# A conv/attention block with a dense mixture of experts: the experts' first layer in f32 on four 64x64 quadrants instead of two f16 halves on 128x64

## The chip, the cores and the metric

The kernel runs on one core of a Trainium2 chip. The metric is device time in microseconds of one execution; lower is better. Three runs of the kernel before took 228.62, 228.63 and 231.39 us, median 228.63 us.

## The reference

x is (4, 64, 64, 16) f32: four images, a column axis of 64 rows (h), and 64 x 16 positions. The first part (a cosine transform, windowed attention, convolutions, inverse transform) gives x1, which is added to x. The second part treats each of the 4 x 1024 positions as a token of 64 features. What the change touches is this second part:

```python
logits = xt @ Wr + br
probs = jax.nn.softmax(logits, axis=-1)
top_p, top_idx = jax.lax.top_k(probs, TOP_K)          # TOP_K = 2
weights = top_p / top_p.sum(axis=-1, keepdims=True)
...
xn = (xt - mu) * jax.lax.rsqrt(var + LN_EPS)
xe = xn[None, :, :] * ln_g[:, None, :] + ln_b[:, None, :]
h = jax.nn.gelu(jnp.einsum('end,edh->enh', xe, W1) + b1[:, None, :], approximate=False)
y = jnp.einsum('enh,ehd->end', h, W2) + b2[:, None, :]
```

There are 8 experts, each 64 -> 256 -> 64. The kernel computes all 8 for every token and weighs them by a gate that is zero for the unchosen ones.

## The kernel before, in words

**Layout.** The four images are two pairs. A pair lies with image and h on the 128 partitions (image 0 on rows 0 to 63, image 1 on rows 64 to 127) and 1024 positions on the free axis. Four "steps" of 512 positions (`CHUNK`) times 8 experts make 32 *units* `u`.

**Order.** `TURN` gives each stage of the first part a turn for pair 0 and for pair 1, and `in_turn` sorts them; every engine walks its own list in that order and waits on semaphores. The units come at turns 90, 100, 110 and so on: `experts(r)` on TensorE first does the second layer of units 2r and 2r+1 (`down`), then the first layer of units 2r+4 and 2r+5 (`up`), since `AHEAD` is 2. Rounds r = -2 and r = -1 have no `down`. Between them, at turns 91 to 94, stand pair 1's `router`, `features`, `keep_tokens` and `tanh_gap`; after r = -1 come `gates_to_rows` and `keep_gates` (101, 102), and SyncE then sends the gates through DRAM and back, copied over the partitions (`store_gates`, `load_gates`).

**First layer before.** A unit has four *tiles* `t`: two halves of the hidden axis (`k`) for each of two images (`b`), each a PSUM bank of 128 hidden rows by 512 tokens. The tokens are split into an f16 high part and an f16 low part, which lie above each other on the 128 partitions (`tok`), so one 128-row matmul multiplies both with the same f16 weights; the weights too are split in two f16 parts (`w1s`), which are accumulated. `up` (L675 to L697) thus issues per tile 2 parts x 2 column sides = 4 f16 matmuls of 128 rows by 64 columns by 512. The split costs `high_part` on ScalarE (L818), `low_part` on GpSimdE (L922), f16 transposes in `features` (L638), copies of 128x1024 f16 in `keep_tokens` (L830), and two more operations in `weights_of_first` (L935, L936).

**Banks.** The first layer has two PSUM banks in the first four units (`h_early`, rounds r = -2 and r = -1, 16 tiles) and six afterwards (`h_late`). Before each tile, `up` waits for the Gelu of the last tile that used this bank. `gelu_hidden` on ScalarE (L852) reads a tile, adds the bias and writes `hid_of[u % 4]`. ScalarE is the only reader.

**Second layer.** `down` (L699) is four f32 matmuls of 128 rows by 64 columns by 512 per unit; VectorE multiplies the result by the gate and adds it (`add_expert`, L1160 and L1165).

An f32 matmul is one row in the order of instructions and two in the trace (two passes); an f32 transpose is one.

Of the kernel before, what the change touches and what calls it, by code (L numbers as in the profile page):

```python
# [15 lines left out]
P = 128  # L16
PAIRS, B2, H, W, C = 2, 2, 64, 64, 16
K = 8
# [4 lines left out]
E, HID = 8, 256  # L23
# [29 lines left out]
    "inverse_over_kh": (35, 40), "keep_back": (24, 27), "keep_half": (25, 28), "square_tokens": (26, 31),  # L53
    "mix_branches": (16, 18), "inverse_over_kw": (36, 41), "high_part": (29, 92), "tokens": (37, 43),
    "residual": (19, 22), "norm_tokens": (21, 24), "keep_tokens": (30, 93), "features": (42, 92), "low_part": (6, 7),
    "router": (39, 91), "route": (23, 25), "gates_to_rows": (101, 102), "shares": (26, 27), "biases": (20, 20),
# [32 lines left out]
def constants():  # L89

    def twice(a):
        return np.kron(np.eye(2), a)
    n = np.arange(H)
    angle = np.cos(np.pi * (2 * n[None, :] + 1) * n[:, None] / (2 * H))
    dct = 2.0 * angle
    weight = np.ones(H)
    weight[0] = 0.5
    idct = (weight[:, None] * angle / H).T
    centred = dct - dct.mean(axis=1, keepdims=True)
    centred[1:] = dct[1:]  # L100
# [19 lines left out]
    return out, np.eye(P, dtype=np.float16)  # L120

# [36 lines left out]

def metaformer(nc, x, small, W1, W1T, ln_b, W2, const32, const16, out):
    ctx = ExitStack()  # L160
    with ctx:
# [36 lines left out]
        c32 = sb("c32", [P, CONST_N])  # L198
        c16 = sb("c16", [P, P], F16)

# [4 lines left out]
        mask = c32[:, CONST["shifted"].start + C:CONST["shifted"].start + C + P]  # L205
        ident16 = c16[:, 0:P]
        sm = sb("sm", [P, SMALL_N])
# [16 lines left out]
        w1g = sb("w1g", [P, E, HID])  # L224
        w1s = sb("w1s", [P, 2, E, HID], F16)
        w2 = sb("w2", [P, NT, H])
# [6 lines left out]
        x1 = sb("x1", [P, PAIRS, N])  # L233
        tok = sb("tok", [P, PAIRS, 2, B2, TT // 2 * P], F16)
        still = sb("still", [P, CHUNK], F16)
# [19 lines left out]
        back = x_conv  # L255
        parts = [x_conv[p].bitcast(F16) for p in range(PAIRS)]
        h2 = [place[4][:, p, :] for p in range(PAIRS)]
# [31 lines left out]

        hid = sb("hid", [P, 2, TILES, CHUNK])  # L290
        hid_of = [hid[:, 0], hid[:, 1]] + [w[:, :, :].rearrange("p (t a) n -> p t (a n)", t=TILES) for w in (w1f, w1g)]
        gate_b = [wide[n][:, 0, :].rearrange("p (e n) -> p e n", n=CHUNK) for n in range(2)]
# [4 lines left out]
        gate_store = nc.dram_tensor("gate_store", (PAIRS, 2, B2, E * CHUNK), F32)  # L297

        def part_of(p, part, j):

            return parts[p].rearrange("p (t a h) -> p t a h", a=2, h=H)[:, j * K:(j + 1) * K, part, :]

        def shifted(p, b, tap):
# [5 lines left out]
        dct_in = sem("dct_in")  # L309
        const_in, const16_in, weights_in = sem("const_in"), sem("const16_in"), sem("weights_in")  # L310
        ffn_in, out_done = sem("ffn_in"), sem("out_done")
# [18 lines left out]
         attn_ready, y_ready, yt_ready, mix_ready, xout_ready, back_ready, half_ready, x1_ready, csq_ready, xn_ready,  # L330
         high_ready, parts_ready, wr_centred_ready, logits_read, tok_ready, gap_ready, tanh_ready, gparts_ready, gates_ready, coef_ready) = (sem(n) for n in (
             "sq_ready dh_ready dw_ready xd_ready h1_ready halo_ready xt_ready gram_ready prod_ready tk_ready "
             "dconv_ready xconv_ready spread_ready scaled_ready h2_ready rest_ready logit_ready exp_ready "
             "attn_ready y_ready yt_ready mix_ready xout_ready back_ready half_ready x1_ready csq_ready xn_ready "
             "high_ready parts_ready wr_centred_ready logits_read tok_ready gap_ready tanh_ready gparts_ready gates_ready coef_ready").split())

# [9 lines left out]
        def _(sp):  # L346
# [5 lines left out]
            sp.dma_start(xs[:, 1, :], xv[1]).then_inc(x_in[1], 16)  # L352
            sp.dma_start(c16[:, :], const16).then_inc(const16_in, 16)
            w1v = W1.rearrange("e d n -> d e n")
# [53 lines left out]
        def _(pe):  # L408
# [229 lines left out]
            def features(p):  # L638

                pe.wait_ge(const16_in, 16)  # L640
                pe.wait_ge(logits_read, p + 1)
                to = slot(p, 1).bitcast(F16)
                for j in range(TT):
                    if j % 4 == 0:
                        pe.wait_ge(parts_ready, 2 * p + j // 4 + 1)
                    for b in range(B2):
                        a = (j // 4 * 2 + b) * CHUNK + j % 4 * P
                        mm = pe.transpose(to[:, a:a + P], parts[p][:, (j * 2 + b) * P:(j * 2 + b + 1) * P], ident16)
                    if j % 4 == 3:
                        mm.then_inc(tok_done, 1)  # L650
# [24 lines left out]
            def up(u):  # L675
# [8 lines left out]
                if u == EARLY:  # L684
                    pe.wait_ge(gates_ready, PAIRS)
                for t in range(TILES):
                    k, b = divmod(t, B2)
                    n = TILES * u + t
                    before = last_in(h_bank, n)
                    if before >= 0:  # L690
                        pe.wait_ge(gelu_ready, before + 1)
                    for part in range(2):
                        for side in range(2):
                            mm = pe.matmul(h_bank(n)[side * H:(side + 1) * H, :],  # L694
                                           w1s[:, part, e, k * P + side * H:k * P + (side + 1) * H], tok[:, pair, half, b, :],
                                           start=part == 0, stop=part == 1)
                    mm.then_inc(w1_done, 1)  # L697

# [32 lines left out]
        def _(act):  # L731
# [85 lines left out]

            def high_part(p):  # L818
                for j in range(2):
                    act.wait_ge(xn_ready, 2 * p + j + 1)  # L820
                    act.copy(part_of(p, 0, j), split(bank(xc[p], j), H)).then_inc(high_ready, 1)  # L821

            def keep_router_weights(p):
# [28 lines left out]
            def gelu_hidden(u):  # L852
# [4 lines left out]
                for t in range(TILES):  # L857
# [6 lines left out]
            stages = (square_columns, keep_router_weights, keep_dw, keep_xd, gelu_in, keep_xt, keep_tk, gelu_depthwise, gelu_out, exponent,  # L864
                      keep_y, keep_yt, keep_back, keep_half, square_tokens, high_part, keep_tokens, tanh_gap, keep_gates)
            for stage, args in in_turn(stages, experts):
# [4 lines left out]
        def _(pool):  # L871
# [49 lines left out]

            def low_part(p):  # L922

                for j in range(2):
                    pool.wait_ge(high_ready, 2 * p + j + 1)
                    pool.tensor_tensor(part_of(p, 1, j), split(bank(xc[p], j), H), part_of(p, 0, j), ALU.subtract).then_inc(parts_ready, 1)  # L926

            def weights_of_first(p):
# [9 lines left out]
            for stage, (p,) in in_turn((weights_of_first, join, high, low_part)):  # L938
                stage(p)
# [252 lines left out]
```

## Time and profile before

| | us |
|---|---|
| median of three runs | 228.63 |
| profiled execution, span from first to last instruction | 227.4 |
| run median less this span | 1.2 |
| TensorE busy | 206.7 (91%) |
| ScalarE busy | 128.1 (56%) |
| VectorE busy | 123.8 (54%) |
| GpSimdE busy | 47.0 (21%) |
| TensorE's share of the chain that ended last | 68% |
| mean granted TensorE clock | 0.981 |

The profile's own record of the execution has no other time than its span, so the 1.2 us between it and the median of the runs is taken as what lies around the span. "PE" is TensorE's matmuls, "PEld" its weight loads, DVE is VectorE, ACT is ScalarE, POOL is GpSimdE. A matmul record (start, duration) lasts longer than the distance to the next one, since matmuls are pipelined: distances between starts give the rate. The chain of waits is followed back from the last instruction and shows what set the end.

### The profile page before, as it was taken

The numbers are of one execution on the slowest core, as the hardware profiler recorded it, in microseconds if no ns is written. First come the engines' busy times: TensorE is split into PE (matmuls) and PEld (weight loads), VectorE is DVE, ScalarE is ACT, GpSimd is POOL, SyncE is SP. The second block draws the span as 40 slices with busy tenths as digits, with TensorE's granted clock in tenths as the row PEclk, the third lists the DMA queues.
The fourth block names the chain that finished last, engine by engine and source line by source line (L and its number), as shares of the span: only waits on it lengthen the run. The fifth ranks groups of instructions, "written<-read, shape, count | busy, mean of one in ns | idle before, by whom it ended". The sixth has DMA issues, their size and how long they took to land.

```text
span 227.4 us, 4913 instructions
## 1 busy us (share of the span) xinstructions
PE 206.7 (91%) x2096; PEld 113.6 (50%) x2096; DVE 123.8 (54%) x232; ACT 128.1 (56%) x207; POOL 47.0 (21%) x50
## 2 busy tenths in 40 slices
PE   7699788999976898988899799999999999999993
PEld 3395667566334577963524244444444444444430
DVE  0582055659949977999731633554334553334555
ACT  2256942035338553669685387666786666786640
POOL 5560393040069992030400000000000000000000
PEclk9979999999999999999699999999999999999998
DMA  6990000000000000000005953260804508063001
GB/s 219 294 265 14 0 3 6 3 0 7 0 0 4 0 3 0 3 0 0 3 0 164 220 128 69 82 151 0 184 3 108 122 4 184 0 150 84 0 0 46
DMA packets 6596, 14.35 MB, mean 63 GB/s; under 512 B 2736, under 2 KB 4144, under 8 KB 5680
## 3 DMA queue, kind: packets, MB, share of 16 engines
q1 hardware_dynamic: 6576, 14.06, 24.7%
q8 instruction: 16, 0.26, 0.5%
q14 instruction: 4, 0.03, 0.0%
HBM read 12.87 MB, written 1.18 MB: 62 GB/s over the span
## 4 chain that ended last, share of the span: by engine, by line
PE 68%; ACT 9%; DMA 7%; POOL 6%; DVE 6%; SPq 1%; issue 1%; POOLq 1%; DVEq 0%
PE psum L710 22%; PE psum L694 21%; PE psum L538 7%; DMA xs<-in_x 3%; DMA wide<-gate_store 2%; PE psum L512 2%; POOL place L920 2%; ACT place L747 2%; PE psum L634 2%; PE psum L548 2%; PE psum L424 2%; POOL place L926 2%; ACT hid L861 1%; POOL place L919 1%; PE psum L557 1%
## 5 line engine op out<-in xcount | busy, mean ns | idle before, releaser
L694 PE MATMUL psum<-tok,w1s 128*64 128x512 f16 x512 | 60.8, 383 | 1.3 <-ACT hid L861 0.8
L1160 DVE SCALAR_TENSOR_TENSOR term<-psum,sm,wide 128x512 f32<-128x512 f32 x32 | 24.0, 750 | 62.1 <-PE psum L710 51.6
L861 ACT ACTIVATE hid<-psum,b1p 128x512 f32<-128x512 f32 x64 | 38.2, 701 | 16.7 <-PE psum L694 16.3
L694 PEld LDWEIGHTS psum<-tok,w1s 128*64 128x64 f16 x512 | 28.7, 110 | 35.9 <-issue 9.1
L861 ACT ACTIVATE w1f<-psum,b1p 128x512 f32<-128x512 f32 x32 | 19.6, 688 | 17.1 <-PE psum L694 17.0
L710 PE MATMUL psum<-hid,w 128*64 128x512 f32 x128 | 28.9, 593 | 0.0
L1165 DVE TENSOR_TENSOR x<-x,term 128x512 f32<-128x512 f32 x32 | 22.1, 692 | 1.1
L861 ACT ACTIVATE w1g<-psum,b1p 128x512 f32<-128x512 f32 x32 | 19.7, 714 | 0.2
L710 PEld LDWEIGHTS psum<-hid,w 128*64 128x64 f32 x128 | 9.1, 137 | 15.1 <-issue 9.4
L710 PE MATMUL psum<-w1g,w 128*64 128x512 f32 x64 | 15.1, 594 | 1.4 <-DVE term L1160 1.4
L538 PE MATMUL psum<-h_pad,tap_bd 64*64 64x512 f32 x144 | 15.9, 589 | 0.0
L710 PE MATMUL psum<-w1f,w 128*64 128x512 f32 x64 | 15.1, 594 | 0.1
L777 ACT ACTIVATE place<-psum 128x512 f32<-128x512 f32 x4 | 2.2, 594 | 15.4 <-PE psum L538 15.4
L538 PEld LDWEIGHTS psum<-h_pad,tap_bd 64*64 64x64 f32 x144 | 6.8, 133 | 7.5 <-issue 7.5
L911 POOL TENSOR_TENSOR place<-place 128x1024 f32<-128x1024 f32 x2 | 4.7, 2353 | 26.0 <-ACT place L777 26.0
L710 PEld LDWEIGHTS psum<-w1g,w 128*64 128x64 f32 x64 | 4.5, 137 | 10.9 <-issue 6.6
L414 PE MATMUL psum<-still 128*128 128x512 f16 x28 | 8.0, 435 | 1.3 <-POOL still L872 1.3
L926 POOL TENSOR_TENSOR place<-place 128x512 f16<-128x512 f32 x4 | 4.6, 1166 | 19.7 <-ACT place L821 19.7
L998 DVE TENSOR_TENSOR wide<-psum,sm 128x1024 f32<-128x1024 f32 x4 | 4.7, 1220 | 7.0 <-PE psum L498 7.0
L735 ACT ACTIVATE place<-psum 128x512 f32<-128x512 f32 x4 | 2.4, 597 | 10.3 <-PE psum L424 10.3
L710 PEld LDWEIGHTS psum<-w1f,w 128*64 128x64 f32 x64 | 4.5, 137 | 6.7 <-issue 3.1
L992 DVE TENSOR_TENSOR wide<-psum,c 128x512 f32<-128x512 f32 x4 | 2.6, 682 | 9.6 <-PE psum L486 9.6
(147 smaller groups left out, 295.4 us busy)
## 6 DMA issues: line engine op xcount, KB each, us to landing
wide<-gate_store SPq DMA_DIRECT2D x14, 512.0 KB, 6.4
xs<-in_x SPq DMA_DIRECT2D x2, 512.0 KB, 5.6
w1f<-in_W SPq DMA_DIRECT2D x2, 512.0 KB, 10.0
block_out<-x SPq DMA_DIRECT2D x4, 256.0 KB, 6.4
wide<-gate_store SPq DMA_DIRECT2D x2, 384.0 KB, 5.1
c<-const SPq DMA_DIRECT2D x1, 548.5 KB, 4.4
hid<-in_W1T SPq DMA_DIRECT2D x1, 512.0 KB, 10.3
w<-in_W SPq DMA_DIRECT2D x1, 512.0 KB, 11.8
```

The lines of the kernel that those rows point to most:

```text
L414: pe.matmul(where, still[:, 0:P], still[:, 0:where.shape[1]], start=True, stop=True)
L424: mm = pe.matmul(slot(p, 0)[:, cp * P:(cp + 1) * P], xs[:, p, cp * P:(cp + 1) * P], dct_h, start=True, stop=True)
L512: mm = pe.matmul(bank(slot(p, 0), swapped)[rows_of(crossed(half, swapped)), 0:side], const("pick")[rows_of(half), first:first + H], column ...
L538: mm = pe.matmul(bank(slot(p, 0), b)[rows_of(crossed(half, b)), :], tap_bd[rows_of(half), tap, :], shifted(p, b, tap)[rows_of(half)], star ...
L694: mm = pe.matmul(h_bank(n)[side * H:(side + 1) * H, :], w1s[:, part, e, k * P + side * H:k * P + (side + 1) * H], tok[:, pair, half, b, :] ...
L710: mm = pe.matmul(y_bank(u)[b * H:(b + 1) * H, :], w2[:, e * KT + k, :], hid_of[u % 4][:, B2 * k + b, :], start=k == 0, stop=k == KT - 1)
L861: act.activation(hid_of[u % 4][:, t, :], h_bank(n), ACT.Gelu, bias=b1p[:, e * KT + k:e * KT + k + 1]).then_inc(gelu_ready, 1)
L911: pool.tensor_tensor(x_conv[p], x_conv[p], xd[p], ALU.add).then_inc(xconv_ready, 1)
L926: pool.tensor_tensor(part_of(p, 1, j), split(bank(xc[p], j), H), part_of(p, 0, j), ALU.subtract).then_inc(parts_ready, 1)
L998: dve.tensor_tensor(prod[p].rearrange("p (s o q) n -> p o s q n", s=2, o=2)[:, j], slot(p, j).rearrange("p (s q n) -> p s q n", s=2, n=P), ...
L1160: dve.scalar_tensor_tensor(term[:, u % 2, :], y_bank(u), b2t[:, e:e + 1], gate_b[part][:, e % (E // 2), :], ALU.add, ALU.mult).then_inc(te ...
L1165: dve.tensor_tensor(x1p, x1p, term[:, u % 2, :], ALU.add).then_inc(add_done, 1)
```

## The change

The tokens stay f32 in the pair's layout: image 0's 64 features on rows 0 to 63, image 1's on rows 64 to 127. The first layer is then, for each k, four f32 matmuls of 64 rows by 64 columns by 512: image by row half, side of the hidden half by column half, with the order (image 0, side 0), (image 1, side 1), (image 0, side 1), (image 1, side 0). `high_part`, `low_part`, `w1s` and the constant `c16` go; `tok` is f32; `features` is 8 f32 transposes for a pair instead of 16 f16 ones; `keep_tokens` copies 128x512 f32. Since `w1g` now stays as the weights, the fourth hidden buffer is a third part of `hid`. `up` waits for both banks of a k before its first matmul.

```diff
-                for t in range(TILES):
-                    k, b = divmod(t, B2)
-                    n = TILES * u + t
-                    before = last_in(h_bank, n)
-                    if before >= 0:
-                        pe.wait_ge(gelu_ready, before + 1)
-                    for part in range(2):
-                        for side in range(2):
-                            mm = pe.matmul(h_bank(n)[side * H:(side + 1) * H, :],
-                                           w1s[:, part, e, k * P + side * H:k * P + (side + 1) * H], tok[:, pair, half, b, :],
-                                           start=part == 0, stop=part == 1)
-                    mm.then_inc(w1_done, 1)
+                moving = bank(tok[:, pair, :], half)
+                for k in range(KT):
+                    first = TILES * u + B2 * k
+                    for b in range(B2):
+                        before = last_in(h_bank, first + b)
+                        if before >= 0:
+                            pe.wait_ge(gelu_ready, before + 1)
+                    for swapped in range(2):
+                        for b in range(B2):
+                            side = crossed(b, swapped)
+                            mm = pe.matmul(h_bank(first + b)[rows_of(side), :],
+                                           w1g[rows_of(b), e, k * P + side * H:k * P + (side + 1) * H], moving[rows_of(b), :],
+                                           start=True, stop=True)
+                            if swapped:
+                                mm.then_inc(w1_done, 1)
...
-                pe.wait_ge(const16_in, 16)
                 pe.wait_ge(logits_read, p + 1)
-                to = slot(p, 1).bitcast(F16)
                 for j in range(TT):
                     if j % 4 == 0:
-                        pe.wait_ge(parts_ready, 2 * p + j // 4 + 1)
-                    for b in range(B2):
-                        a = (j // 4 * 2 + b) * CHUNK + j % 4 * P
-                        mm = pe.transpose(to[:, a:a + P], parts[p][:, (j * 2 + b) * P:(j * 2 + b + 1) * P], ident16)
+                        pe.wait_ge(xn_ready, 2 * p + j // 4 + 1)
+                    mm = pe.transpose(slot(p, 1)[:, j * P:(j + 1) * P], xc[p][:, j * P:(j + 1) * P], ident)
...
-                act.copy(tok[:, p, j, :, :].rearrange("p b n -> p (b n)"),
-                         slot(p, 1).bitcast(F16)[:, j * N:(j + 1) * N]).then_inc(tok_ready, 1)
+                act.copy(bank(tok[:, p, :], j), bank(slot(p, 1), j)).then_inc(tok_ready, 1)
...
-                link(pool.tensor_tensor(w1g[:, :, :], w1f[:, :, :], lng.unsqueeze(2).broadcast_to([P, E, HID]), ALU.mult))
-                link(pool.tensor_copy(w1s[:, 0, :, :], w1g[:, :, :]))
-                pool.tensor_tensor(w1s[:, 1, :, :], w1g[:, :, :], w1s[:, 0, :, :], ALU.subtract).then_inc(w1_ready, 1)
+                pool.tensor_tensor(w1g[:, :, :], w1f[:, :, :], lng.unsqueeze(2).broadcast_to([P, E, HID]), ALU.mult).then_inc(w1_ready, 1)
```

**TensorE from pair 1's `tokens` through round r = -2 to pair 1's `features`, before** (`psum<-c,x` is `tokens`, `psum<-tok,w1s` the first layer, L666 the router, L648 `features`):

```order
L634 MATMUL psum<-c,x 128x128 [waits x1_ready]
L634 MATMUL psum<-c,x 128x128 x3
L694 MATMUL psum<-tok,w1s 64x512 [waits tok_ready,w1_ready,bias_ready]
L694 MATMUL psum<-tok,w1s 64x512 x7
L694 MATMUL psum<-tok,w1s 64x512 [waits gelu_ready]
L694 MATMUL psum<-tok,w1s 64x512 x3
L666 MATMUL psum<-wr_centred,x 128x16 [waits wr_centred_ready,x1_ready]
L666 MATMUL psum<-wr_centred,x 128x16 x7
L648 MATMUL psum<-c,place 128x128 [waits parts_ready,logits_read,const16_in]
L648 MATMUL psum<-c,place 128x128 x7
```

The pair of rows with the wait for `gelu_ready` stands six times there, once for each tile from the third on. With the change:

```order
L625 MATMUL psum<-c,x 128x128 [waits x1_ready]
L625 MATMUL psum<-c,x 128x128 x3
L683 MATMUL psum<-tok,w1g 64x512 [waits tok_ready,w1_ready,bias_ready]
L683 MATMUL psum<-tok,w1g 64x512 x3
L683 MATMUL psum<-tok,w1g 64x512 [waits gelu_ready]
L683 MATMUL psum<-tok,w1g 64x512 x3
L653 MATMUL psum<-wr_centred,x 128x16 [waits wr_centred_ready,x1_ready]
L653 MATMUL psum<-wr_centred,x 128x16 x7
L635 MATMUL psum<-c,place 128x128 [waits xn_ready,logits_read]
L635 MATMUL psum<-c,place 128x128 x3
```

The pair with `gelu_ready` now stands three times, and each stands for two tiles.

**ScalarE over the same stretch, before** (L821 is `high_part`, L833 `keep_tokens`, L816 `square_tokens`, L861 the Gelu, L838 `tanh_gap`):

```order
L821 CAST place<-place 128x8x64 [waits xn_ready] x2
L833 COPY tok<-psum 128x1024 [waits tok_done] x2
L816 ACTIVATE place<-psum 128x512 [waits tokens_done] x2
L861 ACTIVATE hid<-psum,b1p 128x512 [waits w1_done] x8
L838 ACTIVATE st<-st 128x16 [waits gap_ready]
L821 CAST place<-place 128x8x64 [waits xn_ready] x2
L833 COPY tok<-psum 128x1024 [waits tok_done] x2
L838 ACTIVATE st<-st 128x16 [waits gap_ready]
L861 ACTIVATE w1f<-psum,b1p 128x512 [waits w1_done] x4
```

And with the change:

```order
L818 COPY tok<-psum 128x512 [waits tok_done] x2
L806 ACTIVATE place<-psum 128x512 [waits tokens_done] x2
L845 ACTIVATE hid<-psum,b1p 128x512 [waits w1_done] x8
L822 ACTIVATE st<-st 128x16 [waits gap_ready]
L818 COPY tok<-psum 128x512 [waits tok_done] x2
L822 ACTIVATE st<-st 128x16 [waits gap_ready]
L845 ACTIVATE hid<-psum,b1p 128x512 [waits w1_done] x4
```

The casts are gone; pair 1's tanh still stands ahead of the Gelus of round r = -1, and eight Gelus still stand ahead of pair 0's tanh.

## Rows read from the trace of the kernel before

**Rows 1.** Chain of waits, in order of time: start us, us, what.

```profile
130.54 3.45 PE psum L694 x32
133.99 3.43 PE psum L710 x16
...
216.63 6.89 PE psum L710 x32
```

**Rows 2.** Timeline, TensorE, pair 1's taps: start us, us, engine line, operation.

```profile
55.36 7.92 PE L538 MATMUL psum<-h_pad,tap_bd 64*64 64x512 f32 x72
```

**Rows 3.** Groups by line: busy us, mean ns, idle before and its releaser.

```profile
L538 PE MATMUL psum<-h_pad,tap_bd 64*64 64x512 f32 x144 | 15.9, 589 | 0.0
```

**Rows 4.** Timeline, ScalarE, the eight Gelus of one steady round.

```profile
151.73 4.74 ACT L861 ACTIVATE hid<-psum,b1p 128x512 f32<-128x512 f32 x8 [2.15 <-PE psum L694]
```

**Rows 5.** Timeline, TensorE, changes between 64x64, 128x64 and 128x128 tiles.

```profile
28.76 1.09 PE L458 MATMUL psum<-place,enter_bd 64*64 64x512 f32 x8 [0.66 <-ACT place L747]
29.77 1.14 PE L465 MATMUL psum<-place,conv_bd 128*64 128x64 f32 x16
48.58 1.98 PE L548 MATMUL psum<-wide,c 128*128 128x512 f32 x4
50.49 2.10 PE L512 MATMUL psum<-wide,c 64*64 64x64 f32 x128
```

**Rows 6.** Timeline, TensorE, pair 1's inverse transform to pair 1's router.

```profile
95.56 2.00 PE L625 MATMUL psum<-c,place 128*128 128x128 f32 x16
...
99.73 2.00 PE L634 MATMUL psum<-c,x 128*128 128x128 f32 x16
101.66 1.05 PE L694 MATMUL psum<-tok,w1s 128*64 128x512 f16 x8
...
107.01 1.96 PE L666 MATMUL psum<-wr_centred,x 128*128 128x16 f32 x16
```

**Rows 7.** Chain of waits, from pair 0's features to the gates' arrival.

```profile
91.13 0.87 PE psum L608 x8
...
96.95 2.28 POOL place L926 x2
...
103.73 0.70 ACT hid L861
104.43 0.04 issue
104.47 0.64 PE psum L694 x4
105.12 0.02 issue
...
117.18 1.30 ACT w1g L861 x2
118.48 0.18 ACT gate_rows L843 x2
...
127.80 0.76 DVE term L1160
128.60 1.94 PE psum L710 x8
```

**Rows 8.** Timeline, ScalarE, pair 1's tanh and round r = -1.

```profile
112.85 0.22 ACT L838 ACTIVATE st<-st 128x16 f32<-128x16 f32 x1
112.97 2.70 ACT L861 ACTIVATE w1f<-psum,b1p 128x512 f32<-128x512 f32 x4
```

**Rows 9.** Busy us by stretch: PE, PEld, DVE, ACT, POOL, granted clock, DMA share, GB/s.

```profile
7.40:10.80 3.40, 1.20 (x7) 0.51 (x5) 2.35 (x6) 0.00 (x0) 2.34 (x8) 1.00 1.08 259
62.00:65.40 3.40, 2.13 (x14) 0.64 (x7) 1.72 (x2) 1.08 (x2) 0.92 (x1) 1.00 0.00 0
106.40:109.80 3.40, 2.57 (x23) 2.04 (x22) 2.43 (x6) 2.40 (x6) 1.30 (x2) 0.99 0.00 0
109.80:113.20 3.40, 3.34 (x24) 2.04 (x24) 3.09 (x10) 2.27 (x4) 1.01 (x1) 0.50 0.02 5
```

More of the change, by code:

```diff
@@ L53 @@
     "inverse_over_kh": (35, 40), "keep_back": (24, 27), "keep_half": (25, 28), "square_tokens": (26, 31),
-    "mix_branches": (16, 18), "inverse_over_kw": (36, 41), "high_part": (29, 92), "tokens": (37, 43),
-    "residual": (19, 22), "norm_tokens": (21, 24), "keep_tokens": (30, 93), "features": (42, 92), "low_part": (6, 7),
+    "mix_branches": (16, 18), "inverse_over_kw": (36, 41), "tokens": (37, 43),
+    "residual": (19, 22), "norm_tokens": (21, 24), "keep_tokens": (30, 93), "features": (42, 92),
     "router": (39, 91), "route": (23, 25), "gates_to_rows": (101, 102), "shares": (26, 27), "biases": (20, 20),
@@ L119, in constants @@
     out[:, CONST["small_index"]] = np.arange(E, 0, -1)[None, :]
-    return out, np.eye(P, dtype=np.float16)
+    return out
 SMALL = {}
@@ L156, in small_weights, with metaformer @@
     return out
-def metaformer(nc, x, small, W1, W1T, ln_b, W2, const32, const16, out):
+def metaformer(nc, x, small, W1, W1T, ln_b, W2, const32, out):
     ctx = ExitStack()
@@ L233, in metaformer @@
         x1 = sb("x1", [P, PAIRS, N])
-        tok = sb("tok", [P, PAIRS, 2, B2, TT // 2 * P], F16)
+        tok = sb("tok", [P, PAIRS, N])
         still = sb("still", [P, CHUNK], F16)
@@ L255, in metaformer @@
         back = x_conv
-        parts = [x_conv[p].bitcast(F16) for p in range(PAIRS)]
         h2 = [place[4][:, p, :] for p in range(PAIRS)]
@@ L288, in last_in @@
             return max((k for k in range(n) if which(k) is which(n)), default=-1)
-        hid = sb("hid", [P, 2, TILES, CHUNK])
-        hid_of = [hid[:, 0], hid[:, 1]] + [w[:, :, :].rearrange("p (t a) n -> p t (a n)", t=TILES) for w in (w1f, w1g)]
+        hid = sb("hid", [P, 3, TILES, CHUNK])
+        hid_of = [hid[:, 0], hid[:, 1], hid[:, 2], w1f[:, :, :].rearrange("p (t a) n -> p t (a n)", t=TILES)]
         gate_b = [wide[n][:, 0, :].rearrange("p (e n) -> p e n", n=CHUNK) for n in range(2)]
@@ L297, in metaformer @@
         gate_store = nc.dram_tensor("gate_store", (PAIRS, 2, B2, E * CHUNK), F32)
-        def part_of(p, part, j):
-            return parts[p].rearrange("p (t a h) -> p t a h", a=2, h=H)[:, j * K:(j + 1) * K, part, :]
         def shifted(p, b, tap):
@@ L309, in metaformer @@
         dct_in = sem("dct_in")
-        const_in, const16_in, weights_in = sem("const_in"), sem("const16_in"), sem("weights_in")
+        const_in, weights_in = sem("const_in"), sem("weights_in")
         ffn_in, out_done = sem("ffn_in"), sem("out_done")
@@ L330, in metaformer @@
          attn_ready, y_ready, yt_ready, mix_ready, xout_ready, back_ready, half_ready, x1_ready, csq_ready, xn_ready,
-         high_ready, parts_ready, wr_centred_ready, logits_read, tok_ready, gap_ready, tanh_ready, gparts_ready, gates_ready, coef_ready) = (sem(n) for n in (
+         wr_centred_ready, logits_read, tok_ready, gap_ready, tanh_ready, gparts_ready, gates_ready, coef_ready) = (sem(n) for n in (
              "sq_ready dh_ready dw_ready xd_ready h1_ready halo_ready xt_ready gram_ready prod_ready tk_ready "
@@ L816, in square_tokens @@
                     act.activation(bank(squares[p], j), bank(slot(p, 0), j), ACT.Square).then_inc(csq_ready, 1)
[L818 to L821, printed above, removed]
             def keep_router_weights(p):
@@ L864, in _ @@
             stages = (square_columns, keep_router_weights, keep_dw, keep_xd, gelu_in, keep_xt, keep_tk, gelu_depthwise, gelu_out, exponent,
-                      keep_y, keep_yt, keep_back, keep_half, square_tokens, high_part, keep_tokens, tanh_gap, keep_gates)
+                      keep_y, keep_yt, keep_back, keep_half, square_tokens, keep_tokens, tanh_gap, keep_gates)
             for stage, args in in_turn(stages, experts):
@@ L920, in high @@
                     pool.tensor_tensor(bank(rest[p], b), bank(h2[p], b), bank(xd[p], b), ALU.add).then_inc(rest_ready, 1)
[L922 to L926, printed above, removed]
             def weights_of_first(p):
@@ L933, in weights_of_first @@
                 pool.wait_ge(xt_ready, 1)
-                link(pool.tensor_tensor(w1g[:, :, :], w1f[:, :, :], lng.unsqueeze(2).broadcast_to([P, E, HID]), ALU.mult))
-                link(pool.tensor_copy(w1s[:, 0, :, :], w1g[:, :, :]))
-                pool.tensor_tensor(w1s[:, 1, :, :], w1g[:, :, :], w1s[:, 0, :, :], ALU.subtract).then_inc(w1_ready, 1)
-            for stage, (p,) in in_turn((weights_of_first, join, high, low_part)):
+                pool.tensor_tensor(w1g[:, :, :], w1f[:, :, :], lng.unsqueeze(2).broadcast_to([P, E, HID]), ALU.mult).then_inc(w1_ready, 1)
+            for stage, (p,) in in_turn((weights_of_first, join, high)):
                 stage(p)
@@ L1178 @@
     a = {n: np.asarray(v) for n, v in inputs.items()}
-    const32, const16 = constants()
+    const32 = constants()
     arrays = {
@@ L1184 @@
         "in_ln_b": a["L0_ffn_ln_b"].reshape(1, E * H), "in_W2": a["L0_ffn_W2"],
-        "const32": const32, "const16": const16,
+        "const32": const32,
     }
```

6 lines of the change are left out of this document (1 added, 5 removed).

## The prediction

> **What bounds the kernel now.** I read the chain of waits first, then the timelines of TensorE and ScalarE along it, then the busy table by stretch for the clock. From 130.54 us on it is TensorE alone: first layer of two units, 3.45 us, second layer of two units, 3.43 us, by turns, up to two second-layer blocks at the end [rows 1]. ScalarE does the eight Gelus of such a round in 4.74 us and then idles 2.15 us until TensorE delivers again [rows 4]. So late in the kernel only TensorE's rate counts. Before that the chain is another one: between 103 and 118.5 us it alternates between a Gelu on ScalarE (0.70 us) and a tile on TensorE (0.64 us) with 0.06 us of issue, 1.40 us for each turn [rows 7]. There the first layer has two PSUM banks, and each bank's turn is "matmul, then Gelu"; two banks in turn give a tile every 0.70 us. That chain leads to the copies of the gates at 118.48 us, their way through DRAM, and the first gated sum at 127.80 us, which frees TensorE at 128.60 us [rows 7]. Whatever delays the gates moves all that follows.
>
> **Steady rounds: the rate of the matmuls.** What is an f32 matmul on one quadrant worth? The taps are just that: 72 passes of 64x64 by 512 in 7.92 us [rows 2]. With four quadrants at work that is 18 slots; 7.92 less the 0.16 us by which one record (0.589) outlasts a slot gives 0.43 us a slot [rows 2, 3]. The second layer's 16 passes, two column halves at a time, are 8 slots in 3.43 us, 0.43 us as well [rows 1]. The first layer now needs, for two units, 16 f32 matmuls = 32 passes = 8 slots = 3.44 us. Before, 32 f16 passes, two at a time, took 3.45 us [rows 1]. The number of passes is the same; an f32 pass takes twice an f16 one, and four instead of two run side by side. **0.0 us** for each first-layer block after the early rounds.
>
> **Changes of tile shape.** All expert matmuls were 128x64. Now the first layer is 64x64 and the second stays 128x64, so the shape changes twice a round. Where this happens before: L458 starts at 28.76 and the next shape at 29.77, 1.01 us for two slots that should be 0.86, so 0.15 over; L548 takes 1.91 us to the next shape's start for four slots, 1.72, so 0.19 over [rows 5]. From the second layer at 128.60 us to the end there are 13 first-layer blocks, each with a change on both sides: 26. I take 0.15, from the row with 64-column weights, which is nearest: **+3.9 us**, with 0 and 26 x 0.19 = 4.9 as ends. The Trainium skill, "TensorEngine Tiling (Array Packing)", section Key Properties, says that a change of tiling mode, not of tile, drains TensorE. The rows agree in that a change is not free; if the 0.16 us tail of a record came on top of the 0.15 us, the sum would be 4.2 us higher, which is a rival below.
>
> **Steady bank waits.** `up` now waits for both banks of a pair. The fourth pair of a block needs the block's first two Gelus. They are ready 1.09 us (the pair's matmuls, [rows 5]) plus some 0.1 plus 1.30 us (two Gelus, [rows 7]) after the block's start, 2.5 us; the fourth pair is due at 3 x 0.86 + 0.15 = 2.73. Slack 0.2 us, so 0 us; if it fails, 13 x 0.2 is the price. Eight Gelus of 4.74 us still fit into a round of 7.2 us.
>
> **Pair 0's tokens.** ScalarE's casts and GpSimdE's two subtractions (2.28 us, in the chain [rows 7]) go. Eight f32 transposes, by L608 0.87 us [rows 7], can follow L625, which ends at 97.56 [rows 6]; then `tokens` of pair 1 takes 101.66 - 99.73 = 1.93 us as before. Round r = -2 starts at 100.36 instead of 101.66: **-1.3 us**. `keep_tokens` copies shorter rows beside it and is covered by these 1.93 us. GpSimdE's two missing weight operations end by some 45 us before and nobody waits: 0. One small DMA less at the start: 0.
>
> **Early rounds: both banks at once.** Here is the loss. With two banks and a pair of tiles per step, the overlap between TensorE and ScalarE is gone: a step is two Gelus 1.30 (from 117.18, [rows 7]), issue 0.04, a pair of tiles on four quadrants alone 1.09 (L458, two slots and the tail, [rows 5]), issue 0.02: **2.45 us for two tiles** instead of 1.40.
> - Round r = -2: the fourth pair starts at 100.36 + 3 x 2.45 = 107.71, pair 1's router 1.01 us later [rows 5], 108.72 instead of 107.01 [rows 6]: +1.7.
> - VectorE's routing of pair 1 is released by the router, and the tanh by that; ScalarE stands at this tanh, so the tanh moves from 112.85 to 114.55 and the first Gelu of round r = -1 from 112.97 to 114.7 [rows 8]. Pair 1's features, without the subtractions, lie in that time (1.0 us of transposes, two copies) and cost nothing.
> - Round r = -1: 114.7 + 1.30 + 3 x 2.45 = 123.35, and there the gates are copied, 118.48 before [rows 7]: **+4.9 us** against before, the -1.3 included. The DMAs, the first gated sum and the start at 128.60 shift with it. TensorE meanwhile does r = 0's second layer and the next first layer and waits again, as before.
>
> **Clock.** The granted clock was 1.00 in all but two places: it was 0.50 after 7.4 to 10.8 us, where PE was busy 1.20 of 3.40 us, and again at 109.8 to 113.2 us, after a stretch with the router's 16-column matmuls. It held 1.00 through 62.0 to 65.4 us with PE busy 2.13 of 3.40 [rows 9]. In the early steps PE will be busy 1.09 of every 2.45 us, more than before the first fall and less than where it held, and PE waits over 2 us on ScalarE, which stands at the tanh, within r = -1. I expect the lower level (1.2 GHz) once or twice more. At it two slots take up to 0.86 us longer; one low stretch like that of 109.8 to 113.2 holds one or two steps, so 0.9 to 1.7: **+1.3 us**, ends 0 and 5.2 (six steps).
>
> **Sum.** 227.4 + 4.9 + 3.9 + 1.3 = 237.5 us of span. The median of the runs lies 1.2 us over the profiled span of 227.4, so **238.7 us**, 4.4% over 228.63.
>
> **Rivals.**
> 1. *The clock stays at 2.4 GHz in the early rounds.* For it speaks that TensorE works every 2.45 us. 237.4 us, chance 0.28.
> 2. *It is low through both early rounds.* The rows allow it, since the new step lies between the one that fell and the one that held. 227.4 + 4.9 + 3.9 + 5.2 + 1.2 = 242.6 us, 0.12.
> 3. *Not slower: the early pair costs no overlap.* Place: the wait for `gelu_ready` ahead of each pair in rounds r = -2 and -1. The gates' delay is 6 x step - 9.8 us; if TensorE could fill one bank of a pair while the other is read, the step stayed 1.40 and the delay would be -1.4: 227.4 - 1.4 + 3.9 + 1.2 = 231.1 us, +1.1%. It decides below a step of 1.75 us. Against it: both waits stand ahead of the pair's first matmul, in the order of instructions too, and both banks get their last matmul in the same slot. 0.07. With free changes of shape besides, 227.2 us.
> 4. *A change of shape costs a whole drain on top.* 26 x (0.15 + 0.16) = 8.1 us in place of 3.9: 242.9 us. Against it: the over-long intervals above already contain the change. 0.05.
> 5. *The quadrants don't run four at a time.* Two at a time would add 14 x 3.44 = 48 us: 287 us. The taps run in the same four-quadrant order with the same passes, so 0.01.
> 6. *Faster by over 2%*, from something I don't see in ScalarE or the DMA of the gates: 0.02.
>
> My forecast's own case has the remaining 0.45. The **range** is 235.0 to 243.0 us: below it lies rival 3, above it 5 and little of 2 and 4; the lower end allows changes of 0.10 us (-1.3) and some 1 us of the early delay hidden. A measurement of this kernel can tell some 2% from no change, 4.6 us. Faster 0.02, within 2% 0.08, slower 0.90.
>
> **What would show it.** The chain after: first-layer blocks of about 3.6 us and second-layer ones of about 3.6 us, with no ScalarE in the steady part. Early rounds: TensorE groups 2.45 us apart, ScalarE Gelus in twos, and idle ScalarE of about 1.1 us between. Gates copied near 123 us. Granted clock 0.50 somewhere in 103 to 122 us. I am wrong if the steady first-layer block is not 3.4 to 3.7 us, if steps are under 2 us, or if ScalarE stands in the chain in the steady rounds (then the 0.2 us slack failed).

## The result and the profile after

| | kernel before | changed kernel |
|---|---|---|
| median of the runs, us | 228.62 (228.38 to 231.39, 4 runs) | 242.17 (241.60 to 243.27, 4 runs) |
| ratio, 95% interval | | 1.057 (1.051 to 1.063) |
| profiled execution, span, us | 227.4 | 239.8 |
| mean granted clock | 0.981 | 0.962 |

The changed kernel is 5.7% slower. The forecast was 238.7 us with a range of 235.0 to 243.0. Here and below a ratio leaves out runs that lie more than 1.5% above the kernel's fastest, so for own bank and for the common wait on the kernel before, it is not the quotient of the medians.

The chain of waits of the changed kernel over the early rounds and into the steady ones (start us, us, what; L683 is the first layer, L653 the router, L1067 VectorE's reading of the router's result, L635 the features, L845 the Gelu, L700 the second layer):

```profile
99.04 1.09 PE psum L683 x8
100.13 1.26 ACT hid L845 x2
101.39 0.14 issue
101.53 1.15 PE psum L683 x8
...
106.61 1.09 PE psum L683 x8
107.69 2.49 PE psum L653 x16
...
110.21 0.30 DVE place L1067
...
110.55 1.97 PE psum L635 x8
112.52 1.99 PE psum L683 x8
114.51 1.26 ACT hid L845 x2
...
115.90 2.05 PE psum L683 x8
...
124.81 1.25 ACT w1f L845 x2
126.06 0.18 ACT gate_rows L827 x2
...
135.86 0.76 DVE term L1136
...
136.66 1.94 PE psum L700 x8
138.60 3.63 PE psum L683 x32
142.23 3.58 PE psum L700 x16
...
228.81 7.04 PE psum L700 x32
```

Against [rows 7] the single Gelus have become twos, each with a whole pair of tiles behind it, and a step of two tiles takes 2.54 us in round r = -2 (101.53 to 104.06 in the timeline below) and 3.43 us in round r = -1 (115.90 to 119.34), where the pair's matmuls take 2.05 instead of 1.15 us. Between the two rounds the chain goes from the router through pair 1's features (L635) and the first pair of tiles to the first Gelu, all on TensorE but for 0.30 us on VectorE. Against [rows 1] a steady round has grown from 3.45 + 3.43 = 6.88 us to 3.63 + 3.58 = 7.21. ScalarE stands nowhere in the steady chain; its timeline there answers to [rows 4], the same 4.74 us and a longer idle time:

```profile
175.80 4.74 ACT L845 ACTIVATE hid<-psum,b1p 128x512 f32<-128x512 f32 x8 [2.48 <-PE psum L683]
```

The timeline of TensorE of the changed kernel over the same stretch (start us, us, engine, line, operation, idle before) answers to [rows 6]:

```profile
101.53 1.09 PE L683 MATMUL psum<-tok,w1g 64*64 64x512 f32 x8 [1.46 <-ACT hid L845]
104.06 1.09 PE L683 MATMUL psum<-tok,w1g 64*64 64x512 f32 x8 [1.45 <-ACT hid L845]
...
107.62 2.54 PE L653 MATMUL psum<-wr_centred,x 128*128 128x16 f32 x16
...
119.34 1.98 PE L683 MATMUL psum<-tok,w1g 64*64 64x512 f32 x8 [1.45 <-ACT hid L845]
```

Its busy table (busy us of PE, PEld, DVE, ACT, POOL, then the granted clock, DMA share, GB/s) shows where the longer pairs come from:

```profile
103.70:107.10 3.40, 1.58 (x15) 0.47 (x16) 2.21 (x7) 1.49 (x3) 0.00 (x0) 1.00 0.00 0
108.50:109.00 0.50, 0.50 (x6) 0.50 (x5) 0.00 (x0) 0.50 (x2) 0.00 (x0) 0.81 0.00 0
111.10:124.70 13.60, 9.24 (x40) 2.35 (x38) 4.82 (x20) 5.19 (x9) 0.00 (x0) 0.50 0.00 1
136.66:235.80 99.14, 99.14 (x648) 29.13 (x648) 42.36 (x59) 61.59 (x104) 0.00 (x0) 1.00 0.33 77
```

The granted clock falls between 108.5 and 109.0 us, within the router's matmuls and after a round in which TensorE idled 1.45 us in every step, and stays at 0.50 (1.2 GHz) until 125.5 us. Before, it was at 0.50 there from 109.8 to 113.2 us only [rows 9], and the first Gelu of round r = -1 started at 112.97 us [rows 8] instead of 114.51.

The two profiled executions differ by 12.4 us. Place by place, from the starts in the chains and timelines:

| stretch | before | after | difference, us |
|---|---|---|---|
| start to pair 1's inverse transform | 95.56 | 94.39 | -1.2 |
| from there to round r = -2 | 6.10 | 4.58 | -1.5 |
| round r = -2 to the router | 5.35 | 8.65 | +3.3 |
| router to the first Gelu of r = -1 | 5.96 | 6.87 | +0.9 |
| that Gelu to the gates' copy | 5.51 | 11.57 | +6.1 |
| gates' copy to the second layer of unit 3 | 10.12 | 10.60 | +0.5 |
| from there to the last gated sum | 94.95 | 99.21 | +4.3 |

The first row is not put down to the change: in the execution of before the clock was low during the first transform (16 matmuls there took 3.55 us), in that of after it was not (2.05 us), and spans of before measured later lie between 225.6 and 229.3 us.

### The profile page after: what moved, and what is told of

It is laid out like the page before. It is cut to its first block, busy times and chain, and to the rows that moved or that the text cites. A ratio compares the mean times of both kernels' runs of the same rounds, so it can differ in the third digit from the quotient of the medians.

```text
span 239.8 us, 4928 instructions
## 1 busy us (share of the span) xinstructions
PE 213.4 (89%) x2080; PEld 100.8 (42%) x2080; DVE 122.2 (51%) x232; ACT 124.4 (52%) x203; POOL 36.4 (15%) x44
## 4 chain that ended last, share of the span: by engine, by line
PE 70%; ACT 8%; DVE 7%; DMA 6%; POOL 3%; issue 2%; SPq 1%; POOLq 1%; DVEq 0%
PE psum L683 25%; PE psum L700 22%; PE psum L529 6%; ACT hid L845 3%; DMA wide<-gate_store 3%; DMA sm<-in_small 2%; PE psum L653 2%; PE psum L503 2%; ACT place L737 2%; PE psum L539 2%; PE psum L625 2%; POOL place L903 1%; PE psum L548 1%; PE psum L635 1%; PE psum L489 1%
## 5 line engine op out<-in xcount | busy, mean ns | idle before, releaser
L845 ACT ACTIVATE hid<-psum,b1p 128x512 f32<-128x512 f32 x96 | 57.7, 696 | 45.7 <-PE psum L683 45.7
L683 PE MATMUL psum<-tok,w1g 64*64 64x512 f32 x512 | 64.1, 630 | 8.7 <-ACT hid L845 7.3
L700 PE MATMUL psum<-hid,w 128*64 128x512 f32 x192 | 44.8, 603 | 0.4 <-DVE term L1136 0.4
L683 PEld LDWEIGHTS psum<-tok,w1g 64*64 64x64 f32 x512 | 17.0, 136 | 52.7 <-issue 27.2
L700 PEld LDWEIGHTS psum<-hid,w 128*64 128x64 f32 x192 | 12.5, 138 | 31.2 <-issue 29.2
L845 ACT ACTIVATE w1f<-psum,b1p 128x512 f32<-128x512 f32 x32 | 19.6, 714 | 4.3 <-PE psum L683 4.3
L700 PE MATMUL psum<-w1f,w 128*64 128x512 f32 x64 | 15.1, 594 | 1.5 <-DVE term L1136 1.5
L700 PEld LDWEIGHTS psum<-w1f,w 128*64 128x64 f32 x64 | 4.5, 137 | 10.9 <-issue 8.3
L904 POOL TENSOR_TENSOR place<-place 128x512 f32<-128x512 f32 x4 | 6.9, 1727 | 0.3
L903 POOL TENSOR_TENSOR place<-place,coef_rest 128x512 f32<-128x512 f32 x4 | 6.3, 1576 | 0.3
L902 POOL TENSOR_TENSOR place<-place 128x512 f32<-128x512 f32 x4 | 5.6, 1396 | 0.4 <-ACT place L772 0.4
L912 POOL TENSOR_TENSOR w1g<-w1f,sm 128x2048 f32<-128x2048 f32 x1 | 3.6, 3608 | 10.7 <-ACT place L755 10.7
```

The lines of the kernel that those rows point to most:

```text
L683: mm = pe.matmul(h_bank(first + b)[rows_of(side), :], w1g[rows_of(b), e, k * P + side * H:k * P + (side + 1) * H], moving[rows_of(b), :], ...
L700: mm = pe.matmul(y_bank(u)[b * H:(b + 1) * H, :], w2[:, e * KT + k, :], hid_of[u % 4][:, B2 * k + b, :], start=k == 0, stop=k == KT - 1)
L845: act.activation(hid_of[u % 4][:, t, :], h_bank(n), ACT.Gelu, bias=b1p[:, e * KT + k:e * KT + k + 1]).then_inc(gelu_ready, 1)
L902: link(pool.tensor_tensor(bank(h2[p], b), bank(h2[p], b), bank(x_conv[p], b), ALU.add))
L903: link(pool.tensor_tensor(bank(h2[p], b), bank(h2[p], b), coef_rest[:, :], ALU.mult))
L904: pool.tensor_tensor(bank(rest[p], b), bank(h2[p], b), bank(xd[p], b), ALU.add).then_inc(rest_ready, 1)
```

## The experiments

The theory was: the early rounds lose 10 us (3.3, 0.9 and 6.1 in the table) because both banks are waited for, filled and read together, part of it through the lower clock that TensorE's idling brings; and the steady rounds lose 4.3 us to changes of tile shape. The rivals: f32 quadrants are slow as such, or the order of waits costs in the steady rounds too. Each run was timed beside runs of the kernel before on the same chip; ratios are to that kernel.

### Fillers, for the clock

```diff
                     first = TILES * u + B2 * k
+                    if u < EARLY and (u % 2 or k):
+                        hold_clock(5, bank(slot(0, 0), 0))
```

> The changed kernel with five f16 matmuls of zeros (128x128 by 512) ahead of every wait for a pair of banks in the early rounds r = -2 and r = -1, on a PSUM bank that is free there; nothing else is changed. Theory (the clock follows TensorE's idle time): in the changed kernel the granted clock is 0.50 from pair 1's router to the gates' copies and a step of two tiles takes 3.43 us there instead of 2.54. With the fillers (some 1.1 us of the 1.45 us that TensorE idles in a step) the clock stays at 1.00, all steps take about 2.55, the router 1.9 and the gates are copied about 5 us sooner: about 237 us, 2% under the changed kernel. Rival (the low clock is an accident of this execution, or comes from f32 quadrants as such): the steps of round r = -1 stay at 3.4 us with the clock at 0.50, and the time stays at 241 to 243 us.

Measured: 238.92 us (237.67 to 241.06), ratio 1.044 (1.035 to 1.053); four executions with mean clocks of 0.982, 0.982, 0.993 and 1.000 and spans of 238.5, 237.5, 235.6 and 234.7. The timeline of its TensorE in round r = -1:

```profile
115.62 1.09 PE L685 MATMUL psum<-tok,w1g 64*64 64x512 f32 x8 [0.29 <-ACT hid L847]
116.64 1.25 PE L405 MATMUL psum<-still 128*128 128x512 f16 x5
118.16 1.09 PE L685 MATMUL psum<-tok,w1g 64*64 64x512 f32 x8 [0.27 <-ACT hid L847]
```

Steps are 2.54 us instead of 3.43, and the gates are copied at 123.10 us instead of 126.06. All four mean clocks lie above those of the changed kernel's four executions (0.948 to 0.968). So the low clock in the steps came from idling; f32 quadrants as such run at full clock, in the steady rounds too. The expectation was too good: the clock did not stay at 1.00 and the gates came 3.0 us sooner, not 5. The profiled execution still has a low stretch between the router and the first pair of round r = -1 (0.50 from 111 to 114 us) and one after the wait for the first gated sum, so the fillers mend a part, and what is left without any low clock (the execution at 1.000, span 234.7) is still far over the kernel before.

### Each image behind its own bank

```diff
                     for b in range(B2):
                         before = last_in(h_bank, first + b)
                         if before >= 0:
                             pe.wait_ge(gelu_ready, before + 1)
-                    for swapped in range(2):
-                        for b in range(B2):
-                            side = crossed(b, swapped)
+                        for side in range(2):
...
-                            if swapped:
-                                mm.then_inc(w1_done, 1)
+                        mm.then_inc(w1_done, 1)
```

> The changed kernel with another order inside a pair: wait for image 0's bank, its two column sides, then wait for image 1's bank, its two column sides. Only the order of matmuls and waits is changed. Theory (the pair's common wait is what costs in the early rounds): each bank goes round by itself, matmuls 1.09, Gelu 0.70, issue 0.16, about 1.95 us for two tiles instead of 2.54 to 3.43, the gates come 6 x 0.6 = 3.6 us sooner, and more if the clock stays up: 234 to 239 us. In the steady rounds the four quadrants still overlap, since passes on different quadrants overtake each other in the trace of the taps, so a block stays at 3.63 us. Rival 1 (TensorE starts passes strictly in program order): two passes of one quadrant block the next quadrant, only two quadrants overlap and steady blocks grow by up to 3.4 us each, up to 290 us. Rival 2 (the early delay comes from the f32 passes and not from the common wait): steps stay over 2.4 us and the time stays near 242.

Measured: 238.65 us over all four runs (235.97 to 240.35), ratio 1.033 (1.022 to 1.043). Its chain in round r = -2, then in the steady part:

```profile
99.92 0.70 ACT hid L842
100.62 0.04 issue
100.67 1.10 PE psum L681 x4
...
102.53 1.10 PE psum L681 x4
...
133.24 3.59 PE psum L681 x32
```

A step is 1.86 us (100.67 to 102.53) instead of 2.54, so waiting for, filling and ending both banks together costs 0.68 of the 1.14 us by which a step had grown over 1.40, and rival 2 falls. The gates are copied at 120.63 us. The profiled execution is the fastest of the four; their spans are 234.0, 235.0, 238.3 and 238.3 us at mean clocks of 0.978, 0.971, 0.950 and 0.947, and the ratio stands for the first two alone (over all four it is 1.043). The clock is low in this kernel too: the last two steps of the profiled execution took about 2.65 us each. The steady block stays at 3.59 us: rival 1 falls, four passes still run side by side.

### Four banks in the early rounds

```diff
-        h_early = [bank(slot(0, 1), 0), bank(slot(0, 1), 1)]
-        h_late = h_early + [bank(slot(1, 1), 0), bank(slot(1, 1), 1), bank(slot(1, 0), 1), bank(slot(0, 0), 0)]
+        h_early = [bank(slot(0, 1), 0), bank(slot(0, 1), 1), bank(slot(0, 0), 0), y_banks[0]]
+        h_late = h_early[:2] + [bank(slot(1, 1), 0), bank(slot(1, 1), 1), bank(slot(1, 0), 1), h_early[2]]
...
                 pe.wait_ge(gparts_ready, p + 1)
+                pe.wait_ge(gelu_ready, EARLY * TILES)
```

> The changed kernel with four PSUM banks for the first layer in the early rounds instead of two (the two more are pair 0's other slot, free there); the gates' transposes then wait for the sixteenth Gelu. Theory (bank turns bound the early rounds): TensorE fills one pair of banks while ScalarE reads the other, a step is two Gelus, 1.21 to 1.27 us, and round r = -2 and r = -1 are bound by ScalarE; the gates are copied some 8 to 11 us sooner, which includes the clock staying at 1.00 more of the time: 231 to 235 us. Rival (f32 passes or changes of tile shape bound the early rounds, not the banks): steps stay over 2 us and the gain is under 3 us, 239 to 242 us.

Measured: 231.04 us (229.58 to 232.11, 10 runs), ratio 1.008 (1.004 to 1.012). ScalarE's timeline of round r = -2, then the chain up to the gates and in the steady part:

```profile
100.03 4.96 ACT L846 ACTIVATE hid<-psum,b1p 128x512 f32<-128x512 f32 x8 [0.44 <-PE psum L684]
```

```profile
105.99 0.21 DVE place L1068
106.20 0.04 issue
106.25 1.97 PE psum L635 x8
108.22 1.66 PE psum L684 x8
...
114.83 0.14 issue
114.97 0.32 PE psum L661
115.31 0.29 ACT gate_rows L828 x2
...
127.30 3.63 PE psum L684 x32
```

Eight Gelus take 4.96 us, 1.24 us for two tiles: within a round ScalarE is now the bound. Round r = -2 is no longer in the chain at all: up to 106.20 us that runs over VectorE (normalising pair 1's tokens and, L1068, reading its router's result), which the expectation did not name. The gates are copied 10.75 us sooner than in the changed kernel, and 11 of its 13.5 us of loss are gone. This includes the clock: the ten executions have mean clocks of 0.992 to 1.000, and the changed kernel's low stretch had cost 3.6 us. From the start of round r = -2 to the gates' copy it now is 16.42 us, against 27.09 in the changed kernel and 16.82 in the kernel before. What remains, 1% (2.2 us), is about the steady rounds' 4.3 us less these 0.4 and the 1.5 us gained with pair 0's tokens.

### The common wait alone, put on the kernel before

```diff
-                    before = last_in(h_bank, n)
-                    if before >= 0:
+                    before = last_in(h_bank, n + 1 - b)
+                    if b == 0 and before >= 0:
```

> The kernel before with only the common wait: the first layer still is f16 on 128x64 with its split, but before the first tile of each pair it waits for the Gelus of both banks, and the second tile has no wait. Theory: a step of two tiles becomes two Gelus 1.27, issue 0.16, two tiles 1.07 = 2.5 us instead of 1.40 in the early rounds (1.05 to 1.1 us more, six times), so the gates come 6 to 6.5 us later: 234.5 to 236 us, with 1 to 4 us more if the clock falls as well. The steady blocks stay at 3.45 and 3.43 us. Rival (the delay comes from f32 quadrants and changes of shape): 229 to 230 us.

Measured: 232.29 us over all four (231.97 to 237.60), ratio 1.014 (1.006 to 1.021), span of the profiled execution 229.9. Chain:

```profile
102.12 0.64 PE psum L694 x4
...
102.79 1.27 ACT hid L861 x2
104.06 0.04 issue
104.11 0.64 PE psum L694 x4
```

A step grew without any quadrant or change of shape, so the rival falls, but the size was missed: a step is 1.99 us, not 2.5, and the time lies below the expected range. The slowest execution (237.60 us) had a mean clock of 0.947 where the others had 0.992 and 0.993. The f16 tiles are filled one after the other, so the first Gelu starts after 0.64 us and the second tile's 0.43 us lie beside it. On quadrants both tiles of a pair get their last pass in the same slot and the first Gelu starts after 1.15 us. The loss of 1.14 us a step (2.54 - 1.40) thus splits into 0.59 for the common wait (1.99 - 1.40, measured here on f16 tiles) and 0.55 for the rest, which by the chains is mostly finishing together (1.15 us before the first Gelu instead of 0.66) and 0.10 more of issue; behind its own bank a quadrant tile's step loses 0.46 only (1.86 - 1.40).

### Units by turns, on the changed kernel and on the kernel before

```diff
-                if r >= 0:
-                    down(2 * r)
-                    down(2 * r + 1)
-                for u in (2 * (r + AHEAD), 2 * (r + AHEAD) + 1):
-                    if u < UNITS:
-                        up(u)
+                for i in range(2):
+                    if r >= 0:
+                        down(2 * r + i)
+                    if 2 * (r + AHEAD) + i < UNITS:
+                        up(2 * (r + AHEAD) + i)
```

> The changed kernel with the units of a round in another order on TensorE: second layer of unit 2r, first layer of 2r+4, second layer of 2r+1, first layer of 2r+5, instead of two and two. The work is the same, the tile shape changes four times a round instead of twice. Theory (a change of shape costs 0.165 us, from the steady round of 7.21 us against 6.88): a round grows by 0.33 us to 7.54, over 13 rounds 4.3 us: 245.5 to 247.5 us. Rival (the 0.33 us of a round are waits for banks or weight loads and have nothing to do with changes of shape): the time stays within 1 us of the changed kernel, 241 to 243 us, or shrinks.

> The kernel before with the same order by turns; all its expert matmuls are 128x64, so no shape changes anywhere. It is the control for the changed kernel by turns. Theory: a round stays at 6.88 us and the time within 0.7 us of the kernel before, 228 to 229.5 us. Rival (the order by turns itself costs, through waits for Gelus or for the gated sums): a round grows here too, by what the changed kernel's round grows.

Measured: changed kernel by turns 246.72 us (245.65 to 247.48), ratio 1.077 (1.072 to 1.082). Its chain:

```profile
148.33 1.87 PE psum L700 x8
150.19 1.88 PE psum L683 x16
```

Kernel before by turns 227.64 us (226.75 to 230.62, 10 runs), ratio 0.994 (0.990 to 0.997). Its chain:

```profile
118.72 1.73 PE psum L694 x16
...
148.23 1.72 PE psum L710 x8
149.95 1.73 PE psum L694 x16
```

With shapes that change, two more changes make a round 7.50 instead of 7.21 us; with one shape throughout the same order leaves it at 6.89 from start to start, against 6.88. So it is the change of shape: 0.33 us for the first two of a round, 0.29 for the next two, 0.15 to 0.165 us each. What within a change takes that time (the emptying of the array, or the weights for the new shape) was not separated.

A by-product: by turns the kernel before is 0.6% faster. The first layer of unit 5 now lies between the second layers of units 2 and 3 and fills the 1.43 us in which TensorE waited there for the first gated sum (127.80 and 128.60, [rows 7]); in the chain by turns no gated sum stands between the second layers of units 2 and 3.

### Both edits together, and four banks on the kernel before

The changed kernel with own banks and four banks:

> The changed kernel with both: four PSUM banks in the early rounds, and each image's two column sides behind the wait for its own bank. Theory (ScalarE bounds the early rounds once there are four banks): steps stay at 1.21 to 1.27 us and only the first Gelu of a round can start up to 0.5 us sooner; the steady rounds are 7.17 to 7.21 us: 230 to 231 us, within 1 us of four banks alone. Rival (the common wait still costs with four banks): 2 us or more below it.

Measured: 230.22 us (228.77 to 231.09, 10 runs), ratio 1.005 (1.002 to 1.008). Four banks hide the common wait nearly wholly, as expected.

The kernel before with four banks (the edit above on its own lines):

> The kernel before with four PSUM banks for the first layer in the early rounds and the gates' transposes behind the sixteenth Gelu. Theory (there a step of two tiles already is 1.40 us, near the 1.21 to 1.27 us that two Gelus take): 6 x 0.15 = 0.9 us is gained and about 0.4 us lost, since the gates' transposes no longer run beside the last Gelu: 228.0 to 228.8 us, no difference to be measured. Rival (the four banks by themselves are worth the 8 to 11 us that they gave the changed kernel): 218 to 221 us.

Measured: 228.83 us (227.77 to 231.10, 12 runs), ratio 1.000 (0.997 to 1.003). Its chain between the two rounds (L822 is `high_part`, L927 `low_part`):

```profile
106.11 0.63 ACT place L822
...
106.81 1.15 POOL place L927
```

Four banks are worth 11 us to the changed kernel and nothing to the kernel before; they repair a loss that the pairs made. That it is nothing, and not the 0.9 us of the expectation, has a reason in the split: round r = -2 is over sooner (the router starts 3.69 us after it instead of 5.35), but then TensorE waits 2.27 us for GpSimdE's part of pair 1's tokens. From the start of round r = -2 to the gates' copy it is 16.87 us, against 16.82 before. The 1.2 us by which the next expectation takes the gates to come sooner is the earlier start of round r = -2 in this execution (100.19 against 101.66 us) and no gain of the four banks.

The kernel before with four banks and by turns:

> The kernel before with both edits that left its f16 first layer alone: units by turns, and four PSUM banks in the early rounds. By turns alone it was 0.6% faster than before, since in the trace the first layer of unit 5 now stands between the second layers of units 2 and 3 and fills the 1.43 us in which TensorE waited for the first gated sum. Four banks alone copied the gates some 1.2 us sooner, of which little arrived. Theory (the gates' way through DRAM sets the start of the steady rounds, and both edits shorten the wait for it): about 0.5 us under by turns alone, 226.8 to 227.6 us, ratio 0.990 to 0.994. Rival (once the 1.43 us are filled, TensorE's own work sets the end, and the gates' earlier copy moves nothing): the same as by turns alone, 227.4 to 228 us. Either way it should not be slower than the kernel before.

Measured: 227.68 us (226.13 to 228.63, 7 runs), ratio 0.993 (0.990 to 0.996). It is faster than the kernel before by as much as by turns alone (0.994), within the intervals, which fits the rival; whether four banks add anything here stays open.

## Why the prediction held, and what was off

- *Steady matmul rate, 0.0 us.* Right. The first-layer block is 3.63 us, of which 3.44 is eight slots of 0.43; f32 on four quadrants has no faster rate than f16 in two parts on two column halves.
- *Changes of shape, +3.9 us for 26.* Right in mechanism, measured +4.3 for the same stretch, 0.165 us each, and shown by doubling them on the changed kernel (+0.29 us a round) and on the kernel before (+0.01). Rival 4, a whole drain on top (0.31 us), is out. The Trainium skill, "TensorEngine Tiling (Array Packing)", section Key Properties, says that a change of tiling mode drains TensorE; the cost measured here is of the size of a record's 0.16 us tail, once.
- *Steady bank waits, 0.* Right: TensorE is busy for 99.14 of the 99.14 us from 136.66 us on, ScalarE's eight Gelus take 4.74 us of a 7.21 us round, and it isn't in the chain.
- *Pair 0's tokens, -1.3 us.* Measured -1.5.
- *Early rounds, step 2.45 us, gates +4.9.* Right in mechanism; the step was 2.54, since the chain shows 0.14 us from the last Gelu to the pair's matmuls where I had taken 0.04 from a chain of f16 tiles. Six steps make 0.5 us. That own banks (1.86) and four banks (1.24) shorten the step shows the cause. Rival 3, no loss of overlap, fell: it needed steps below 1.75.
- *Clock, +1.3 us.* This is the term that was mis-sized, and it makes 2.3 of the miss of 3.5 us. I expected one or two low stretches; the profiled execution was at 0.50 without a break from 109.0 to 125.5 us. It came with 0.9 us more between router and first Gelu and 3 x 0.89 = 2.7 us in the steps of round r = -1, 3.6 us in all. It is rival 2 (242.6 us) in half of its place: round r = -2 ran at the full clock. I had priced one stretch of 3.4 us as in the kernel before; but a step at the low clock leaves TensorE idle for the same 1.45 us again, and here the low level lasted until after the last of these steps. What ends it is not known: TensorE worked from 110.55 to 114.44 us without idling and the clock stayed low, and by turns the changed kernel had one pair of 1.09 us between two of 1.99 in that round. Why it differs between executions stays open.
- *The path from the router to the first Gelu of round r = -1.* The path was wrong, though its time came near (5.98 us forecast, 6.87 measured, the difference being the clock's 0.9). I had it through VectorE's routing and pair 1's tanh, with the features beside it at no cost. The tanh came 5.71 us after the router's start, 0.1 sooner than before, but ScalarE then idled 0.94 us until TensorE, at the low clock, had done the features (1.97 us) and the first pair (1.99). ScalarE's timeline shows it:

```profile
113.33 0.22 ACT L822 ACTIVATE st<-st 128x16 f32<-128x16 f32 x1 [0.19 <-DVE st L1088]
114.49 1.27 ACT L845 ACTIVATE hid<-psum,b1p 128x512 f32<-128x512 f32 x2 [0.94 <-PE psum L683]
```

  That the tanh was not later, though the router took 0.58 us longer, comes from two operations of VectorE in between: before, beside GpSimdE's subtraction, they took 0.47 and 0.81 us, now 0.29 each. The chain of before, too, did not alternate between Gelu and tile all the way from 103 to 118.5 us, as I wrote: from 107.8 to 113.1 us it runs through the tanh of pair 0, a cast, GpSimdE's subtraction, the features and a token copy.
- *Around the span, +1.2 us.* It was 2.0 us (241.81 less 239.8). The 1.2 came from setting the median of three runs against the span of another, slower execution; where time and span are of the same execution of the kernel before, they differ by 2.2 to 2.5 us. This and the gates' way through DRAM (+0.5 us, not explained) make the rest, against a start that happened to be 1.2 us shorter.

## What to carry to other kernels

When two tiles are packed into one group, look at the buffers before the matmul rate: with two banks the group turned "fill one, read one" into "fill both, read both" and four banks took 11 us back (some 3.6 of it through the clock), while the rate of the matmuls stayed the same. Count the changes of tile shape between neighbouring blocks, here 0.165 us each, and give a packed group twice the banks that a single tile had. Then look for the next bound: here it was VectorE's work on the tokens, and in the kernel before the split on ScalarE and GpSimdE, which left four banks nothing to gain. A forecast should treat idle time of TensorE on a long chain as a price of its own, since the lower clock makes each later step longer and keeps the idle time.

## What the runs showed of the hardware

- Four quadrants stayed busy in both orders of the four matmuls of a group that were run: with the two column sides of an image next to each other, each matmul being two passes, a steady block took 3.59 us, even 0.04 less than in the crossed order. In the trace the first passes of all four start within 0.02 us; whether passes overtake each other or are issued in that order wasn't separated.
- The same kernel's clock varies between executions: with fillers, mean clocks of 0.982 to 1.000 went with spans of 238.5 to 234.7 us.
- At a granted clock of 0.50 the pair of tiles took 1.99 us instead of 1.09, and the router's 16 narrow matmuls, low throughout in the changed kernel by turns, 3.59 instead of 1.96. The same kernel's clock thus decides several us: own bank took 234.0 us of span at a mean clock of 0.978 and 238.3 at 0.947.
- VectorE's operation of 128x128 f32 took 0.81 us while GpSimdE's subtraction ran (L1103, L926, kernel before) and 0.29 us in the changed kernel, which has no such subtraction. The overlap is what the trace shows; the cause was not tested.
